# SyncE's queue in a recurrent delta-rule stage: kn is stored ahead of beta and loaded ahead of v's stores

## Chip, core and metric

The kernel runs on one core of one Trainium2 chip. The metric is the device time of one execution in microseconds (us); lower is better. Two versions are compared by the medians of their timed runs on the same chip.

## What is computed

A stack of four layers on x of 8 sequences, 256 tokens and 128 features. Each layer is a conditioning step, an attention-like step, a second conditioning step and a feed-forward step, with residual additions. The change lies in the attention-like step of layer 2, a recurrent delta rule with 8 heads of 32, which is fed by an LSTM and followed by a plain RNN. Cut to what matters:

```python
def _L2_attn_ref(x, W_in, W_k, W_v, W_q, W_beta, b_beta, W_out):
    xp = silu(einsum('btd,ed->bte', x, W_in))
    k_all, v_all, q_all = proj(W_k), proj(W_v), proj(W_q)
    beta_all = sigmoid(proj(W_beta) + b_beta)
    def step(S, inp):
        k, v, q, beta = inp
        kn = k / (norm(k) + 1e-06)
        retrieved = einsum('bhij,bhj->bhi', S, kn)
        delta = v - retrieved
        S = tanh(beta[..., None] * S + delta[..., None] * kn[..., None, :])
        Sq = einsum('bhij,bhj->bhi', S, q)
        return S, Sq * silu(Sq)
    S_final, outs = scan(step, S0, (k_all, v_all, q_all, beta_all))
    return einsum('btm,dm->btd', cell_out, W_out)

x = x + _L2_attn_ref(_L2_cond_ref(x, cond, ...), ...)      # LSTM, then the delta rule
x = x + _L2_ffn_ref(_L2_cond2_ref(x, cond, ...), ...)      # plain RNN, then a ternary feed-forward
```

## The kernel before

The program goes through its stages one after the other; all weights lie in SBUF. The stage of the change is `recurrent_stages` (tensor names begin with `l2r_`). It runs three recurrences side by side, each delayed against the one that feeds it. Time is cut into 16 waves of `TC` = 16 steps, and a loop over bodies works on five waves at once (`waves`, L349):

- wave k of the LSTM (`lstm_products`, `lstm_gates`, `lstm_cell`), one step per step of the body;
- wave k-1 of `project`: from the LSTM's output it makes k, v, beta and q of 16 steps in one go, spread over the steps of the body;
- wave k-2 of the delta recurrence: `values` and `retrieve` (L415, L429) put v minus the retrieved value into `d_ps` on TensorE; `masked` (L800) copies it to `rows` on VectorE; `spread_delta` (L441) multiplies it with `outer`, which holds kn, into `o_ps`; `kept` (L649) makes beta times state on GpSimd; `summed` (L808) adds both into `pre` on VectorE; `new_state` (L556) takes the tanh on ScalarE. Each waits for the one before it, so a step is a ring through four engines;
- wave k-3 of the output projection and wave k-4 of the RNN.

TensorE also does matmuls whose result nobody reads (`unread`, L448), a fixed number in each step.

Each engine's instruction order is written out by hand: the code of a step of the body stands in one fixed order on each engine, and every engine executes its own list in order.

k, v and beta come out of `project` with the token (sequence and step) on the partition axis, and the recurrence needs the head and the sequence there. They are turned round through device memory by SyncE's DMA queue. For wave w of `project`, this is:

- `store_beta` (L939): 8 DMAs of 16 KB, from `beta_tok`, once ScalarE's sigmoid of beta (L592, step 9 of the body) is done;
- `store_kn` (L948): 2 DMAs of 64 KB, from `kn_tok`, once GpSimd's multiply (L702, step 9 of the body too) is done;
- `store_v` (L968): 2 DMAs of 96 KB, from `v_part`, in rows of 32 bf16 elements;
- `load_kn` (L957): 4 DMAs of 32 KB to `kn_rows`, once both kn stores have landed. ScalarE multiplies them by a mask into `outer` (L612), four instructions in steps 13 to 15 of the same body, ahead of that step's `new_state`;
- `load_beta` (L927): 16 DMAs of 256 KB to `beta_f`, in four parts of four. The first part and half of the second follow in the same body, the rest in the next, each paced by the step in which its ring slot comes free;
- `load_v` (L976): 1 DMA of 192 KB to `v_rows`, once both v stores have landed. TensorE's `values` of the next body's step 0, at the end of this body, waits for it.

Before this, at the start of each body, SyncE issues the remaining beta loads of the wave that the delta recurrence is in. A wait of a function stands on SyncE ahead of its DMAs and holds up all that is queued behind it.

Of the kernel before, what the change touches and what calls it, by code (L numbers as in the profile page):

```python
# [260 lines left out]
def recurrent_stages(nc, tag, x, y, wx, wh, bias, w_in, w_tok, w_q, beta_bias, w_out, sel_v, mask_r, mask_k, mask_q, mask_l, gate_sel,  # L261
# [8 lines left out]
    with ExitStack() as stack:  # L270
# [78 lines left out]
        def waves(k):  # L349
            return [w if 0 <= w < NTC else None for w in (k, k - 1, k - 2, k - 3, k - 4)]  # L350

        with nc.Block() as block:
# [562 lines left out]
            def _(sp):  # L915
                def load_beta(w, part, chunks, delta=None, step=0):
                    q = w * (TC // QUARTER) + part
                    sp.wait_ge(s["beta_stored"], 16 * B * (w + 1))
                    if q >= BETA_SLOTS:
                        sp.wait_ge(s["bs_ready"], (q - BETA_SLOTS + 1) * QUARTER * 2)  # L920
                        sp.wait_ge(beta_loaded[q % BETA_SLOTS], 16 * 4 * (q // BETA_SLOTS))
                    for m in chunks:
                        if delta is not None and delta * TC + step >= 1:
                            sp.wait_ge(s["bs_ready"], 2 * (delta * TC + step))
                        step += 1
                        here = beta_store[w % 2, :, m, part * QUARTER:(part + 1) * QUARTER].rearrange("g t h b i -> g (t h b i)")
                        sp.dma_start(beta_f[chunk_rows(m), q % BETA_SLOTS].rearrange("p g t h b i -> p g (t h b i)"),  # L927
                                     here.unsqueeze(0).broadcast_to([32, HG, QUARTER * 2 * BH * N2])).then_inc(beta_loaded[q % BETA_SLOTS], 16)

                def store_beta(w):  # L930
                    sp.wait_ge(s["beta_done"], w + 1)
                    if w >= 2:
                        for slot in range(BETA_SLOTS):
                            last = ((w - 1) * (TC // QUARTER) - 1 - slot) // BETA_SLOTS + 1
                            sp.wait_ge(beta_loaded[slot], 16 * 4 * last)
                    if w >= 1:
                        sp.wait_ge(s["beta_stored"], 16 * B * w)
                    for b in range(B):
                        sp.dma_start(beta_store[w % 2, :, :, :, b // BH, b % BH, :].rearrange("g m t i -> t (g m) i"),  # L939
                                     beta_tok[TC * b:TC * (b + 1), :].rearrange("p (c i) -> p c i", i=N2)  # L940
                                     ).then_inc(s["beta_stored"], 16)

                def store_kn(w):
                    sp.wait_ge(s["kn_ready"], w + 1)
                    if w >= 1:
                        sp.wait_ge(s["kn_loaded"], 16 * 4 * w)
                    for h in range(2):
                        sp.dma_start(kn_store[h].rearrange("m b t j -> (b t) m j"), kn_tok[BH * TC * h:BH * TC * (h + 1), :, :]  # L948
                                     ).then_inc(s["kn_stored"], 16)

                def load_kn(w):
                    sp.wait_ge(s["kn_stored"], 16 * 2 * (w + 1))
                    if w >= 1:
                        sp.wait_ge(s["outer_ready"], 4 * w)
                    for c in range(4):
                        h, g = divmod(c, 2)
                        sp.dma_start(kn_rows[32 * c:32 * c + 16, :, :].rearrange("p t j -> p (t j)"),  # L957
                                     kn_store[h, 4 * g:4 * (g + 1)].rearrange("m b t j -> (m b) (t j)")
                                     ).then_inc(s["kn_loaded"], 16)

                def store_v(w):
                    sp.wait_ge(s["top_ready"], w + 1)
                    sp.wait_ge(s["mid_ready"], w + 1)
                    sp.wait_ge(s["v_split"], w + 1)
                    if w >= 1:
                        sp.wait_ge(s["v_loaded"], 16 * w)
                    for h in range(2):
                        sp.dma_start(v_store[:, h].rearrange("r b t i -> (b t) r i"),  # L968
                                     v_part[BH * TC * h:BH * TC * (h + 1), :, :].rearrange("p a (m i) -> p (a m) i", i=N2)
                                     ).then_inc(s["v_stored"], 16)  # L970

                def load_v(w):
                    sp.wait_ge(s["v_stored"], 16 * 2 * (w + 1))
                    if w >= 2:
                        sp.wait_ge(s["d_psum"], (w - 1) * TC)
                    sp.dma_start(v_rows[0:V_ROWS, w % 2, :, :, :].rearrange("p b t i -> p (b t i)"),  # L976
                                 v_store.rearrange("r h b t i -> (r h) (b t i)")).then_inc(s["v_loaded"], 16)

                for k in range(1, NTC + 2):
                    lstm, proj, delta, out, rnn = waves(k)  # L980
                    if delta is not None:
                        load_beta(delta, 1, (2, 3), delta, 0)
                        load_beta(delta, 2, range(4), delta, 2)
                        load_beta(delta, 3, range(4), delta, 6)
                    if proj is not None:
                        store_beta(proj)
                        store_kn(proj)
                        store_v(proj)
                        load_kn(proj)
                        load_beta(proj, 0, range(4), delta, 10)  # L990
                        load_v(proj)
                        load_beta(proj, 1, (0, 1), delta, 14)
# [2233 lines left out]
```

## Time and profile before

| | |
|---|---|
| median of 3 runs | 2966.37 us (2957.95 to 2966.97) |
| the profiled execution's own time | 2981.45 us |
| its span | 2979.7 us |
| mean granted clock of TensorE in it, as a share of full speed | 0.821 |
| busy: PE, DVE, ACT, POOL | 2485.5, 1725.2, 1105.3, 750.8 us |
| SyncE's beta, kn and v stores: first and last issue | 1310.4 and 2070.2 us |

The profile names engines PE (TensorE matmul), PEld (TensorE weight load), DVE (VectorE), ACT (ScalarE), POOL (GpSimd) and SP (SyncE). A row of a timeline merges neighbouring instructions of one line and gives their start, their length together, and in square brackets the idle time of the engine before them with what ended it. For DMAs the length is that of issuing them on SyncE's queue, and "to landing" is the time from an issue to its semaphore. The stage lies between about 1250 and 2180 us of the span.

### The profile page before, as it was taken

How to read it: one execution, taken by the hardware profiler on the slowest of the kernel's cores; microseconds unless marked ns; L12 is line 12 of the kernel's file. 1: busy time of each engine (PE TensorE's matmuls, PEld its weight loads, DVE VectorE, ACT ScalarE, POOL GpSimd, SP SyncE). 2: the span in 40 equal slices, each digit the busy share in tenths (PEclk: the TensorE clock that was granted, in tenths of full speed). 3: DMA queues.
4: the chain of work that ended last, by engine and by line, in shares of the span. 5: the costliest groups of instructions: out<-in, count | busy, mean ns of one | idle time of the engine just before them, and what ended most of it. 6: DMA issues, size and time to landing. Idle time of an engine off the chain costs nothing. (4 is left out here: it accounts for less than half of the span.)

```text
span 2979.7 us, 92693 instructions
## 1 busy us (share of the span) xinstructions
PE 2485.5 (83%) x37349; PEld 1762.4 (59%) x37354; DVE 1725.2 (58%) x7330; ACT 1105.3 (37%) x3986; POOL 750.8 (25%) x1227
## 2 busy tenths in 40 slices
PE   5998888882799889778888888889956878999998
PEld 3556666662455566555666666665534556777774
DVE  3553555556354544347777877776343865566675
ACT  1332333333133223224555555555244433333332
POOL 2210000000221000126666666767333310000000
PEclk9996555555699779889999999999556975898999
DMA  2000000001000000123534343435010000000000
GB/s 89 2 3 2 2 2 2 2 2 39 1 2 2 1 0 0 67 48 92 111 95 108 97 106 98 107 96 115 30 43 1 2 1 2 2 3 2 2 3 15
DMA packets 110106, 103.98 MB, mean 35 GB/s; under 512 B 90496, under 2 KB 90496, under 8 KB 108800
## 3 DMA queue, kind: packets, MB, share of 16 engines
q1 hardware_dynamic: 109696, 98.24, 13.1%
q8 instruction: 291, 4.77, 0.7%
q14 instruction: 119, 0.97, 0.1%
HBM read 89.81 MB, written 8.39 MB: 33 GB/s over the span
## 5 line engine op out<-in xcount | busy, mean ns | idle before, releaser
L649 POOL TENSOR_TENSOR l2r_beta_s<-l2r_state,l2r_beta_f 128x256 f32<-128x256 f32 x512 | 366.1, 736 | 274.8 <-ACT l2r_state L556 265.4
L556 ACT ACTIVATE l2r_state<-l2r_pre 128x256 f32<-128x256 f32 x512 | 191.6, 417 | 220.3 <-DVE l2r_pre L808 218.6
L808 DVE TENSOR_TENSOR l2r_pre<-l2r_o_ps,l2r_beta_s 128x256 f32<-128x256 f32 x512 | 193.1, 418 | 35.2 <-PE l2r_o_ps L441 33.1
L140 PE MATMUL l0r_bank<-main_x,l0r_wx_half 128*128 128x32 f32 (+2 forms) x480 | 150.0, 413 | 60.5 <-ACT l0r_out_gate L196 59.9
L140 PEld LDWEIGHTS l0r_bank<-main_x,l0r_wx_half 128*128 128x128 f32 x480 | 118.7, 311 | 81.7 <-ACT l0r_out_gate L196 79.5
L1801 PEld LDWEIGHTS l3r_bank<-main_x,l3r_wx_half 128*128 128x128 f32 x480 | 98.1, 231 | 93.2 <-issue 49.4
L441 PE MATMUL l2r_o_ps<-l2r_rows,l2r_outer 32*128 32x128 f32 x2048 | 134.1, 333 | 4.6 <-DVE l2r_rows L800 4.1
L194 ACT ACTIVATE l0r_gates<-l0r_bank 128x24 f32<-128x24 f32 x256 | 48.9, 191 | 237.0 <-PE l0r_bank L152 237.0
L1940 ACT ACTIVATE l3r_gates<-l3r_bank 128x24 f32<-128x24 f32 x256 | 48.9, 191 | 232.2 <-PE l3r_bank L1813 232.1
L228 DVE SCALAR_TENSOR_TENSOR l0r_both<-l0r_gates 128x16 f32<-128x16 f32 x256 | 44.8, 175 | 152.4 <-ACT l0r_gates L194 152.4
L152 PE MATMUL l0r_bank<-l0r_h_ring,l0r_w_part 128*128 128x8 bf16 x2304 | 102.6, 170 | 35.7 <-DVE l0r_h_ring L238 28.0
L1784 POOL TENSOR_SCALAR main_y<-l3r_h_ring 128x128 f32<-128x128 f32 x16 | 8.5, 530 | 481.9 <-DVE l3r_h_ring L2094 481.9
L152 PEld LDWEIGHTS l0r_bank<-l0r_h_ring,l0r_w_part 128*128 128x128 bf16 x2304 | 81.5, 105 | 68.4 <-DVE l0r_h_ring L238 65.0
L124 POOL TENSOR_SCALAR main_y<-l0r_h_ring 128x128 f32<-128x128 f32 x16 | 10.3, 645 | 441.8 <-DVE l0r_h_ring L238 441.8
L800 DVE TENSOR_TENSOR l2r_rows<-l2r_d_ps,main_even_layers 128x128 f32<-128x128 f32 x257 | 74.8, 291 | 80.5 <-PE l2r_d_ps L429 75.4
L448 PE MATMUL l2r_d_ps<-l2r_w_part 128*128 128x384 bf16 x384 | 120.8, 359 | 0.0
L441 PEld LDWEIGHTS l2r_o_ps<-l2r_rows,l2r_outer 32*128 32x128 f32 x2048 | 83.5, 191 | 55.5 <-DVE l2r_rows L800 48.0
L429 PE MATMUL l2r_d_ps<-l2r_state,l2r_kq 128*32 128x128 f32 x2056 | 114.2, 284 | 1.6 <-ACT l2r_state L556 1.4
L2084 DVE SCALAR_TENSOR_TENSOR l3r_both<-l3r_gates 128x16 f32<-128x16 f32 x256 | 44.4, 173 | 114.1 <-ACT l3r_gates L1940 113.3
L1314 DVE TENSOR_REDUCE l1a_block_top<-l1a_s_ps 128x6 f32<-128x768 f32 x64 | 61.3, 958 | 83.1 <-PE l1a_s_ps L1167 83.1
L1801 PE MATMUL l3r_bank<-main_x,l3r_wx_half 128*128 128x32 f32 (+2 forms) x480 | 95.9, 295 | 15.4 <-ACT l3r_out_gate L1942 14.8
L1314 DVE TENSOR_REDUCE l0a_block_top<-l0a_s_ps 128x6 f32<-128x768 f32 x64 | 61.3, 958 | 79.6 <-PE l0a_s_ps L1167 79.6
(590 smaller groups left out, 7305.4 us busy)
## 6 DMA issues: line engine op xcount, KB each, us to landing
l2r_beta_f<-l2r_beta_store SPq DMA_DIRECT2D x256, 256.0 KB, 3.3
main_odd_layers<-in_l SPq DMA_DIRECT2D x1, 4826.5 KB, 14.1
main_odd_layers<-in_l SPq DMA_DIRECT2D x1, 3672.0 KB, 16.3
l2r_v_store<-l2r_v_part SPq DMA_DIRECT2D x32, 96.0 KB, 3.5
l2r_v_rows<-l2r_v_store SPq DMA_DIRECT2D x16, 192.0 KB, 7.0
main_decay<-in_decay SPq DMA_DIRECT2D x1, 3072.0 KB, 10.2
main_even_layers<-in_l SPq DMA_DIRECT2D x1, 2762.5 KB, 9.7
l2r_beta_store<-l2r_beta_tok SPq DMA_DIRECT2D x128, 16.0 KB, 1.6
```

The costliest lines, as they stand in the source:

```text
L140: nc.tensor.matmul(into, wx_half[:, g * P:(g + 1) * P], x_b[:, :, w * LW + lo:w * LW + hi].rearrange("p b t -> p t b"), start=False, stop= ...
L152: last = nc.tensor.matmul(ifg(n, at, at + 1), w_part[part][:, g * P:(g + 1) * P], h_parts[k], start=False, stop=(k == 2), skip_group_check ...
L194: nc.scalar.activation(gates[:, 0:3 * B], ifg(n), ACT.Tanh).then_inc(s["gates_ready"], 1)
L429: last = nc.tensor.matmul(d_ps[chunk_rows(c), 0:P], kq[:, n % SLOTS, c, :, :, :].rearrange("p a b c -> p (a b c)"), state[:, c * P:(c + 1) ...
L441: last = nc.tensor.matmul(o_ps[:, c, 0:P], outer[chunk_rows(c), n // TC % 2, n % TC, :, :].rearrange("p a b -> p (a b)"), rows[chunk_rows( ...
L448: nc.tensor.matmul(into[:, P:CHUNK], w_part[0][:, 0:P], w_part[0][:, 0:3 * P], start=True, stop=True)
L556: nc.scalar.activation(state[:, h * 2 * P:(h + 1) * 2 * P], pre[:, h * 2 * P:(h + 1) * 2 * P], ACT.Tanh).then_inc(state_ready[h], 1)
L649: nc.gpsimd.tensor_tensor(beta_s[:, half].rearrange("p (g r) -> p g r", g=HG), state[:, half].rearrange("p (g r) -> p g r", g=HG), beta_f[ ...
L800: nc.vector.tensor_tensor(rows[:, n % SLOTS, :, :].rearrange("p a b -> p (a b)"), d_ps[:, 0:P], mask_r, ALU.mult).then_inc(s["row_ready"], 1)
L808: nc.vector.tensor_tensor(pre[:, half].rearrange("p (c n) -> p c n", c=2), o_ps[:, 2 * h:2 * h + 2, 0:P], beta_s[:, half].rearrange("p (c ...
L1314: nc.vector.tensor_reduce(block_top[:, :, 2 * p:2 * p + 2, r].rearrange("p n g -> p g n"), s_ps[:, :, 0:SPAN].rearrange("p g (n k) -> p g ...
L1801: nc.tensor.matmul(into, wx_half[:, g * P:(g + 1) * P], x_b[:, :, w * LW + lo:w * LW + hi].rearrange("p b t -> p t b"), start=False, stop= ...
```

## The change

In SyncE's loop over the bodies the kn stores stand ahead of the beta stores, and the kn loads stand ahead of the v stores. Nothing else is changed; each function keeps its waits.

```diff
                     if proj is not None:
+                        store_kn(proj)
                         store_beta(proj)
-                        store_kn(proj)
+                        load_kn(proj)
                         store_v(proj)
-                        load_kn(proj)
                         load_beta(proj, 0, range(4), delta, 10)
                         load_v(proj)
                         load_beta(proj, 1, (0, 1), delta, 14)
```

On SyncE, in body 1 (wave 0's projection, the first of the stage), the difference of the two instruction lists is:

```order
 L914 UNCONDITIONAL_BRANCH
+L948 DMA l2r_kn_store<-l2r_kn_tok 64x8x32 x2
 L939 DMA l2r_beta_store<-l2r_beta_tok 16x8x32 x8
-L948 DMA l2r_kn_store<-l2r_kn_tok 64x8x32 x2
+L957 DMA l2r_kn_rows<-l2r_kn_store 16x512 x4
 L968 DMA l2r_v_store<-l2r_v_part 64x24x32 x2
-L957 DMA l2r_kn_rows<-l2r_kn_store 16x512 x4
 L927 DMA l2r_beta_f<-l2r_beta_store 32x2x1024 x4
 L976 DMA l2r_v_rows<-l2r_v_store 48x2048
 L927 DMA l2r_beta_f<-l2r_beta_store 32x2x1024 x12
```

The kn stores moved past the eight beta stores, and the kn loads past the two v stores. The v stores now stand directly ahead of beta's first four loads. The same piece repeats in all 16 bodies that project a wave. In the last of them, body 16, SyncE's list before is:

```order
L939 DMA l2r_beta_store<-l2r_beta_tok 16x8x32 x8
L948 DMA l2r_kn_store<-l2r_kn_tok 64x8x32 x2
L968 DMA l2r_v_store<-l2r_v_part 64x24x32 x2
L957 DMA l2r_kn_rows<-l2r_kn_store 16x512 x4
L927 DMA l2r_beta_f<-l2r_beta_store 32x2x1024 x4
L976 DMA l2r_v_rows<-l2r_v_store 48x2048
```

and after it:

```order
L948 DMA l2r_kn_store<-l2r_kn_tok 64x8x32 x2
L939 DMA l2r_beta_store<-l2r_beta_tok 16x8x32 x8
L957 DMA l2r_kn_rows<-l2r_kn_store 16x512 x4
L968 DMA l2r_v_store<-l2r_v_part 64x24x32 x2
L927 DMA l2r_beta_f<-l2r_beta_store 32x2x1024 x4
L976 DMA l2r_v_rows<-l2r_v_store 48x2048
```

Here too the v load is the last of the wave's six groups that the next body waits for. The lists of TensorE, VectorE, ScalarE and GpSimd are the same in both kernels.

## Rows read from the trace of the kernel before

**Rows 1.** The page, its first line.
```profile
span 2979.7 us, 92693 instructions
```

**Rows 2.** Waits of ScalarE, then of SyncE's queue: us in total, times, longest us.
```profile
ACT l2r_outer L612 <- DMA l2r_kn_rows<-l2r_kn_store: 12.0, 9, 3.3
...
SPq L957 <- DMA l2r_kn_store<-l2r_kn_tok: 1.3, 4, 0.8
```

**Rows 3.** Timeline of SyncE in wave 8's projection: start us, us, DMAs.
```profile
1714.18 3.77 SPq L939 DMA_DIRECT2D l2r_beta_store<-l2r_beta_tok  x8
1718.05 1.27 SPq L948 DMA_DIRECT2D l2r_kn_store<-l2r_kn_tok  x2
1719.48 1.48 SPq L968 DMA_DIRECT2D l2r_v_store<-l2r_v_part  x2
1721.06 3.18 SPq L957 DMA_DIRECT2D l2r_kn_rows<-l2r_kn_store  x4
1724.40 1.73 SPq L927 DMA_DIRECT2D l2r_beta_f<-l2r_beta_store  x4
1726.23 0.36 SPq L976 DMA_DIRECT2D l2r_v_rows<-l2r_v_store  x1
```

**Rows 4.** Timeline of ScalarE and GpSimd in the same wave.
```profile
1713.75 0.40 ACT L592 ACTIVATE l2r_beta_tok<-l2r_beta_tok 128x256 f32<-128x256 f32 x1
...
1714.19 0.61 POOL L702 TENSOR_TENSOR l2r_kn_tok<-l2r_k_tok,l2r_inv 128x256 f32<-128x256 f32 x1
```

**Rows 5.** Windows: us; busy PE, PEld, DVE, ACT, POOL; clock, DMA share, GB/s.
```profile
1720.00:1721.00 1.00, 0.92 (x11) 0.55 (x11) 0.79 (x5) 0.64 (x3) 1.00 (x3) 1.00 0.64 91
1721.00:1722.00 1.00, 0.74 (x25) 0.75 (x26) 0.97 (x5) 0.43 (x2) 1.00 (x3) 1.00 0.93 123
1722.00:1723.00 1.00, 1.00 (x20) 0.58 (x17) 0.84 (x3) 0.54 (x4) 1.00 (x3) 1.00 0.68 81
1726.00:1733.00 7.00, 6.34 (x122) 4.59 (x121) 4.10 (x22) 4.72 (x17) 6.37 (x10) 1.00 1.05 212
```

**Rows 6.** Lines L968, L976 (waves 8 and 2) with landings; L415 taking those v rows.
```profile
L968 SPq DMA_DIRECT2D l2r_v_store<-l2r_v_part x2: 575/716/857, 1719.5 to 1720.1; - x2
...
DMA to landing us min/median/max: 3.2/3.9/4.7
...
L976 SPq DMA_DIRECT2D l2r_v_rows<-l2r_v_store x1: 362/362/362, 1726.2 to 1726.2; - x1
...
DMA to landing us min/median/max: 7.3/7.3/7.3
...
1735.45 0.24 PE L415 MATMUL l2r_d_ps<-l2r_v_rows,l2r_selv_bf 128*32 128x128 bf16 x4
...
L976 SPq DMA_DIRECT2D l2r_v_rows<-l2r_v_store x1: 362/362/362, 1424.4 to 1424.4; - x1
...
DMA to landing us min/median/max: 7.2/7.2/7.2
...
1432.11 0.24 PE L415 MATMUL l2r_d_ps<-l2r_v_rows,l2r_selv_bf 128*32 128x128 bf16 x4
```

**Rows 7.** Timeline of ScalarE around its wait of wave 14, in body 15.
```profile
2026.53 0.75 ACT L556 ACTIVATE l2r_state<-l2r_pre 128x256 f32<-128x256 f32 x2 [0.90 <-DVE l2r_pre L808]
...
2030.16 0.72 ACT L612 ACTIVATE l2r_outer<-l2r_kn_rows,main_even_layers 128x512 f32<-128x512 f32 x1 [2.04 <-DMA l2r_kn_rows<-l2r_kn_store]
...
2030.94 0.71 ACT L556 ACTIVATE l2r_state<-l2r_pre 128x256 f32<-128x256 f32 x2
```

**Rows 8.** Timeline of TensorE: the v rows of waves 0 and 15 are taken.
```profile
1329.05 0.24 PE L415 MATMUL l2r_d_ps<-l2r_v_rows,l2r_selv_bf 128*32 128x128 bf16 x4 [1.38 <-DMA l2r_v_rows<-l2r_v_store]
...
2083.09 0.24 PE L415 MATMUL l2r_d_ps<-l2r_v_rows,l2r_selv_bf 128*32 128x128 bf16 x4 [1.62 <-DMA l2r_v_rows<-l2r_v_store]
```

**Rows 9.** Windows, columns as in rows 5: before and after the clock falls.
```profile
2073.00:2085.10 12.10, 10.34 (x118) 6.38 (x113) 4.26 (x12) 5.87 (x15) 9.25 (x15) 1.00 0.90 195
2085.20:2125.00 39.80, 39.80 (x291) 19.90 (x289) 16.52 (x44) 12.51 (x36) 16.15 (x23) 0.50 0.17 55
```

## The prediction

> **What bounds the kernel now.** I read the page first, for the span [rows 1], then the waits of ScalarE, then the DMA queue of SyncE in order of time. The profiled execution has a span of 2979.7 us and took 2981.45 us; the median of the three timed runs is 2966.37 us, 15.1 us below it. I work out a difference on the profiled execution and add it to the median. A change below 0.3% (8.9 us) can't be told from none here: the three runs alone spread over 9.0 us.
>
> The stage that changes has 20 bodies of 16 steps, about 50 us each once all waves run; body w+1 projects, stores and loads wave w. Its steps are a ring TensorE, VectorE, ScalarE, GpSimd, and SyncE only feeds it. So SyncE's order counts only where an engine of the ring waits for a transfer. I look at three such places.
>
> 1. ScalarE scales the kn rows into `outer` (L612) at step 13. It waited there 9 times in 16 waves, 12.0 us in all [rows 2]. This is the wait the change aims at. The queue itself hardly waits for the kn stores (1.3 us in 4 times, in the same group), so taking the v stores out from between store and load costs it little.
> 2. TensorE's `values` (L415), first of the next body, needs the v rows. It was held up visibly at two of the 16 loads, the first and the last [rows 8].
> 3. GpSimd's `kept` (L649) needs beta's first part.
>
> **The wave in detail, and the same wave after the change.** This is wave 8 before [rows 3]: beta stores at 1714.18, kn stores at 1718.05, v stores at 1719.48, kn loads at 1721.06, beta loads at 1724.40, v load at 1726.23. The beta stores begin as soon as beta's sigmoid (L592) ends, at 1714.15; kn_tok (L702) is ready only at 1714.19+0.61 = 1714.80 [rows 4]. With the kn stores first, the whole queue starts 0.65 us later. Then, with the same durations:
> - kn stores 1714.83 to 1716.10, beta stores 1716.20 to 1719.97 (their landing is no condition for what follows),
> - kn loads from 1720.05 instead of 1721.06, that is **1.0 us earlier** (1.48+0.11 us of v stores taken out, less 0.65 of late start), to 1723.23,
> - v stores 1723.35 to 1724.83, instead of 1719.48,
> - beta loads from 1724.95, **0.55 us later**,
> - v load after both the beta loads (1726.7) and the landing of the v stores. The second v store is issued some 0.6 us after the first and lands 3.2 to 4.7 us later [rows 6]: 1727.3 to 1728.7. So the v load leaves 1.1 to 2.5 us later than its 1726.23.
>
> No transfer, packet or instruction is added or removed, and TensorE, VectorE, ScalarE and GpSimd keep their order. The beta loads of the running wave, ahead of these, keep theirs too.
>
> **What the earlier kn loads bring.** At most the waits in [rows 2], each shortened by about 1.0. Part of each is free: where ScalarE isn't held up at L612, it waits 0.90 us for `pre` in a step, and behind the wait of wave 14 that idle time is gone [rows 7]. Wave 14 has the dearest that isn't tied to the v load: 2.04 us, and its step took 2030.94-2026.53 = 4.41 us [rows 7]; two steps later the pace was normal. Of the 1.0 us I count 0.9. Wave 4 (1.17 us) I count at 0.2, the waits below 0.9 us at nothing. In wave 0, the first, L612 waited 3.26 us, but the body ends with TensorE waiting 1.38 us for v rows at 1329.05 [rows 8], so a faster ScalarE only waits longer there; there the queue starts no later, since kn_tok is ready first, and I count 0.1. In wave 1 the v rows are as close behind, see below. **Gain: 1.2 us.** Its bounds are 0 (every wait hidden) and 8.5 us (1.0 us or the whole wait in each of the nine, all on the path; about 3 us of it from wave 0).
>
> **What the later v and beta loads cost.** The beta loads and the v load keep the DMA engines full: a share of 1.05 in the 7 us from 1726 [rows 5]. The v rows of wave 8 land 7.3 us after their issue [rows 6], at 1733.5, behind beta's. TensorE takes them at 1735.45: 1.9 us to spare. In wave 2 they land at 1424.4+7.2 = 1431.6, and are taken at 1432.11: 0.5 us to spare [rows 6]. Read the same way, the loads of waves 1, 3 and 4 have 0.6 to 0.7, wave 7 has 0.9, the other nine between 1.3 and 2.4, and waves 0 and 15 none.
>
> How much later do they land? Beta's loads are issued 0.55 us later. Besides, the v stores' packets now lie directly ahead of them. Before, these took the engines at shares of 0.64, 0.93 and 0.68 in the three microseconds after 1720 [rows 5], 2.25 us of all sixteen, and were gone when beta's data came, because the kn loads lay between. After, v's data run from some 0.7 to 3.5 us after their issue, 1724.0 to 1726.8, and beta's would begin 1.1 us after its issue, at 1726.0. What is left of v's data then is about a third of them, 0.7 us. So the v rows land 0.55+0.7 = **1.25 us later**. Bounds: 0.55 (no queueing) and 2.8 (0.55 and all 2.25). I take the lower half because most of v's data drain while beta's loads are being issued.
>
> The Trainium skill (DMA: Bandwidth & Descriptors, Anatomy of one DMA) fits a transfer issued by GpSimd as about 2.0 us and its bytes at 436 GB/s; for two v stores of 96 KB each that would be 0.45 us of engine time. The 2.25 us [rows 5] speak against it here, at 64 bytes a packet. By the page nothing of v would be left in beta's way, the shift would be 0.55 us and the whole sum about 0.
>
> With 1.25 us, wave 1 is 0.6 late, wave 2 0.7, waves 3 and 4 0.5 each, wave 7 0.3: 2.6 us. Wave 14, sped up by its kn gain, finds its v rows late and gives back 0.5. Wave 15 already waits, 1.62 us [rows 8], so there the shift counts in full, with its stores also in the way: 1.4 us. **Cost: 4.5 us.** Beta's first part would be late only with 1.5 us or more; it is covered by v, which lands behind it.
>
> **Sum:** -1.2+4.5 = +3.3 us, so about **2970 us**.
>
> **The clock.** TensorE's granted clock is full (2.4 GHz) through the stage and fell to half (1.2 GHz) at body 17, the last with a delta: 1.00 before 2085.1, 0.50 in the 40 us behind it [rows 9], just behind the wait of 1.62 us for wave 15's v rows. The changed kernel makes that wait longer, so I expect the same fall, at most a few microseconds earlier. If some of the timed runs keep full clock there, the change can cost them that. I charge nothing.
>
> **The rivals.**
> - *The v rows come late in nearly every wave* (slower). If v's 64-byte packets keep beta's data back by more than I take, or land late and so delay the v load's own issue, the shift passes 1.9 us. Then six or more further waves lose their slack. At 2.2 us the sum is about +14 us: **2981 us**. It counts as slower from a shift of 1.9 us on (+9 us). For it: a v store took up to 4.7 us to land [rows 6], and the engines are full. Against it: the waves with 1.3 to 2.4 us to spare. Chance 0.20.
> - *ScalarE's wait is on the path* (faster). If a held-up ScalarE delays the ring one for one and the v rows land no later, 8.5 us go: **2958 us**. For it: 4.41 us for the step of wave 14. Against: the 0.90 us of slack [rows 7], which covers four of the nine waits whole. Chance 0.08, of which I give 0.06 to faster by over 0.3%.
> - *It does nothing:* kn lands 1.0 us earlier where nobody waits, v lands later within its slack. **2966 us**. For it: 14 of 16 v loads have slack now. Chance 0.25.
> - The forecast, a few microseconds lost at waves 1 to 4 and 15: 0.47.
>
> **The numbers.** Faster 0.06; slower 0.20; the rest, 0.74, is within 0.3%. The range takes in the faster rival's 2958 below (also the fastest run shown) and the slower one's 2981 above: 2958 to 2982.
>
> **What would show it.** In the profile after: SyncE's first kn store of wave 8 about 0.65 us behind the end of L592, kn loads about 1.0 us earlier and beta loads about 0.5 us later against L592; ScalarE's wait at L612 down from 12.0 to between 2 and 5 us; L415 waiting for the v rows at five to seven loads, not two, 0.3 to 1.5 us each; bodies 5 to 13 as long as before to within 0.7 us. I am wrong if the v rows land more than 2 us later, if bodies get shorter by 0.5 us or more, or if another stage changes.

## The result, and the profile after

| | kernel before | changed kernel |
|---|---|---|
| median of 20 runs each | 2959.79 us | 2977.18 us |
| ratio of the changed kernel to the kernel before | | 1.0071, 95% interval 1.005 to 1.0093 |
| the profiled execution: its own time, its span | 2981.45, 2979.7 us | 2975.27, 2973.4 us |
| mean granted clock of TensorE in it | 0.821 | 0.822 |

The change makes the kernel slower by 0.7%: 21 us by the ratio (15 to 28 by its interval), 17.4 us by the medians. Ratios and the counts further down leave out the executions more than 1.5% above the fastest of their kernel (5938.07 and 3004.14 us of the kernel before and 3881.32 us of the changed one here, three more of the kernel before and one of not15 later). The forecast was 2970 us; 2977.18 us lies inside the stated range, but on the side to which I gave a chance of 0.20. And the two profiled executions show the opposite: the one of the changed kernel is 6 us shorter. Each number of this section has to be read with that in mind.

The queue of SyncE first, in the changed kernel, wave 8 again, with the engine rows that release it. Columns: start us, us, what.

```profile
1712.01 0.40 ACT L592 ACTIVATE l2r_beta_tok<-l2r_beta_tok 128x256 f32<-128x256 f32 x1
...
1713.09 1.27 SPq L948 DMA_DIRECT2D l2r_kn_store<-l2r_kn_tok  x2
1714.53 3.82 SPq L939 DMA_DIRECT2D l2r_beta_store<-l2r_beta_tok  x8
1718.45 2.99 SPq L957 DMA_DIRECT2D l2r_kn_rows<-l2r_kn_store  x4
1721.60 1.49 SPq L968 DMA_DIRECT2D l2r_v_store<-l2r_v_part  x2
1723.25 2.22 SPq L927 DMA_DIRECT2D l2r_beta_f<-l2r_beta_store  x4
1726.20 0.31 SPq L976 DMA_DIRECT2D l2r_v_rows<-l2r_v_store  x1
```

Counted from the start of L592, the queue begins at 1.08 us instead of 0.43 [rows 3, 4], the kn loads at 6.44 instead of 7.31, the beta loads at 11.24 instead of 10.65, the v load at 14.19 instead of 12.48. So the kn loads leave 0.9 us earlier, the beta loads 0.6 us and the v load 1.7 us later, all close to what was worked out. This v load took 7.0 us to land, so the v rows came 1.4 us later.

The waits of ScalarE and TensorE for DMAs in the changed kernel (us in total, times, longest us):

```profile
PEld l2r_d_ps L415 <- DMA l2r_v_rows<-l2r_v_store: 9.8, 5, 4.4
PE l2r_d_ps L415 <- DMA l2r_v_rows<-l2r_v_store: 8.2, 4, 4.1
...
ACT l2r_outer L612 <- DMA l2r_kn_rows<-l2r_kn_store: 1.7, 2, 1.0
```

The 12.0 us of ScalarE [rows 2] are down to 1.7, in 2 waves instead of 9. TensorE now waits for v rows at five loads: its matmuls at four (waves 0, 1, 11 and 15), and a weight load (PEld) alone at wave 14, for 0.37 us. What that makes of the stage is seen from the delta recurrence's tanh (L556), whose row gives its first and last start; before, then after:

```profile
L556 ACT ACTIVATE l2r_state<-l2r_pre x512: 399/417/428, 1331.2 to 2141.5; 128x256 f32<-128x256 f32 x171
```

```profile
L556 ACT ACTIVATE l2r_state<-l2r_pre x512: 416/417/424, 1328.3 to 2141.5; 128x256 f32<-128x256 f32 x171
```

That is 810.3 us and 813.2 us: 2.9 us more, where the sum of the prediction said 3.3. The other 9 us between the two spans lie outside the recurrence. So in this pair of executions the sum comes out (by which terms is looked at further down), and the 21 us of the runs are not to be seen in it. The reason stands in the two rows of the changed kernel that answer to [rows 8, 9]:

```profile
2081.88 0.24 PE L415 MATMUL l2r_d_ps<-l2r_v_rows,l2r_selv_bf 128*32 128x128 bf16 x4 [2.36 <-DMA l2r_v_rows<-l2r_v_store]
```

```profile
2085.20:2125.00 39.80, 39.80 (x291) 19.85 (x289) 16.23 (x43) 12.35 (x36) 16.15 (x23) 0.50 0.17 54
```

TensorE waits 2.36 us instead of 1.62 for wave 15's v rows, and behind it the clock is at half (1.2 GHz), as in [rows 9]. The first question was therefore whether [rows 9] show what the kernel before usually does: its profiled execution took 2981.45 us, 22 us more than the median of 20 runs.

### The profile page after: what moved, and what is told of

Read it like the earlier page. It is cut to its first block and busy times, and to the rows that moved or that the text cites. A ratio compares the mean times of both kernels' runs of the same rounds, so it can differ in the third digit from the quotient of the medians.

```text
span 2973.4 us, 92698 instructions
## 1 busy us (share of the span) xinstructions
PE 2481.7 (83%) x37354; PEld 1760.2 (59%) x37354; DVE 1726.2 (58%) x7330; ACT 1105.8 (37%) x3986; POOL 750.7 (25%) x1227
## 5 line engine op out<-in xcount | busy, mean ns | idle before, releaser
L556 ACT ACTIVATE l2r_state<-l2r_pre 128x256 f32<-128x256 f32 x512 | 192.1, 418 | 231.7 <-DVE l2r_pre L808 229.7
L124 POOL TENSOR_SCALAR main_y<-l0r_h_ring 128x128 f32<-128x128 f32 x16 | 10.3, 645 | 439.3 <-DVE l0r_h_ring L238 439.3
## 6 DMA issues: line engine op xcount, KB each, us to landing
main_odd_layers<-in_l SPq DMA_DIRECT2D x1, 3672.0 KB, 16.2
```

Source lines behind the costliest of these rows:

```text
L556: nc.scalar.activation(state[:, h * 2 * P:(h + 1) * 2 * P], pre[:, h * 2 * P:(h + 1) * 2 * P], ACT.Tanh).then_inc(state_ready[h], 1)
```

## The experiments

Two theories. **Clock:** most executions of the kernel before keep full clock through body 17, since TensorE's wait for wave 15's v rows is short enough; the change makes this wait longer, so the clock is lost nearly always. **Queue:** the v rows come late in many waves, and the pair of traces happens not to show it (my slower rival).

Each experiment comes with 12 runs, against 33 to 35 runs of the kernel before on the same chip, in three sets (to fill15, to load15, the rest). The last column counts the executions whose mean granted clock is 0.827 or lower: among the traces, the highest mean with the clock lost in body 17 is 0.827, the lowest with it kept is 0.828. Only the traced executions show where the clock fell; for the others the mean is a sign of it, and with so narrow a gap a count can be off by one or two.

| kernel | median us | ratio to before, 95% interval | low mean clock |
|---|---|---|---|
| before (three sets) | 2956.52, 2958.2, 2953.45 | | 21 of 102 |
| the change | 2977.18 | 1.0071 (1.005 to 1.0093) | 19 of 19 |
| b_again | 2958.74 | 1.0014 (0.9987 to 1.0042) | 3 of 12 |
| only15 | 2978.19 | 1.0071 (1.0044 to 1.0097) | 11 of 12 |
| not15 | 2963.9 | 1.0006 (0.9979 to 1.0032) | 3 of 11 |
| fill15 | 2957.71 | 0.9994 (0.9972 to 1.0017) | 0 of 12 |
| after_fill15 | 2964.15 | 1.0015 (0.9994 to 1.0036) | 1 of 12 |
| idle15 | 2973.36 | 1.0039 (1.0013 to 1.0066) | 9 of 12 |
| store15 | 2972.3 | 1.0036 (1.001 to 1.0062) | 9 of 12 |
| load15 | 2976.05 | 1.0051 (1.002 to 1.0083) | 12 of 12 |
| vfirst15 | 2955.01 | 0.9985 (0.996 to 1.0009) | 0 of 12 |
| fill_0_15 | 2946.84 | 0.9972 (0.9948 to 0.9995) | 0 of 12 |
| new0_fill | 2947.26 | 0.9969 (0.9947 to 0.9991) | 0 of 12 |
| after_fill_all | 2953.26 | 0.9983 (0.9957 to 1.0008) | 0 of 12 |

**b_again: a second trace of the kernel before.** No edit.

> The kernel before once more, unchanged, for a second trace. Its three first times and its profiled one (2981 us) lie 15 us apart. Clock theory: in a typical execution TensorE keeps full clock in body 17 (the last delta body), and its steps take about 2.7 us there, not 3.57 as in the trace shown; then this profile shows it, if its own time is near 2960 us. Queue theory (the loss of the change sits in v rows that come late in many waves): body 17 looks as in the first trace, at half clock, whatever the time. Both: ratio to before 1.00 within 0.3%.

Its profiled execution took 2950.37 us, 31 us less than the first. Three rows of it: the taking of wave 15's v rows, a window of 40 us in body 17 (columns as in rows 5), and the tanh.

```profile
2073.05 0.24 PE L415 MATMUL l2r_d_ps<-l2r_v_rows,l2r_selv_bf 128*32 128x128 bf16 x4 [0.59 <-DMA l2r_v_rows<-l2r_v_store]
```

```profile
2075.50:2115.50 40.00, 37.69 (x408) 20.49 (x408) 20.98 (x56) 16.22 (x48) 22.16 (x32) 1.00 0.19 58
```

```profile
L556 ACT ACTIVATE l2r_state<-l2r_pre x512: 403/417/428, 1324.1 to 2115.6; 128x256 f32<-128x256 f32 x171
```

The wait is 0.59 us instead of 1.62, the clock stays at 1.00, and 40 us hold 408 matmuls instead of 291 in 39.8 us. The recurrence takes 791.5 us, 18.8 us less than in the first trace of the same program. Most of that is body 17: from its first tanh to its last it takes 40.05 us instead of 55.85, at 2.67 us a step instead of 3.57. So the kernel has two courses, and the profile before the change showed the rarer one (21 of 102). The timed runs put the same price on it: in the three sets the median of the kernel before's executions with a low mean clock lies 18.6, 19.0 and 16.2 us above that of its others.

**only15 and not15: where the loss sits.** The new order in body 16 alone, or in all bodies but that:

```diff
-                    if proj is not None:
+                    if proj is not None and proj == 15:
+                        store_kn(proj)
                         store_beta(proj)
-                        store_kn(proj)
-                        store_v(proj)
                         load_kn(proj)
+                        store_v(proj)
+                    elif proj is not None:
...
```

> The new order of SyncE's queue in body 16 alone (wave 15's projection), the old one in all others. Clock theory: this alone lengthens TensorE's wait for wave 15's v rows from 1.6 to about 3 us and so costs the clock of body 17 nearly always: nearly the whole loss, +12 to +20 us. Queue theory: +1 to +2 us, the shift of one v load.

> The new order in all bodies but body 16. Clock theory: +0 to +6 us, the late v rows of wave 1 and a few others and the half clock behind them in body 3. Queue theory: +15 us or more, the whole loss but for one load.

One body out of 16 carries the loss as far as the intervals can tell: 1.0071 like the change itself, while the other 15 give 1.0006 (at most 1.0032, or 9.5 us). The taking of wave 15's v rows in only15, and 40 us of body 17:

```profile
2076.15 0.30 PE L415 MATMUL l2r_d_ps<-l2r_v_rows,l2r_selv_bf 128*32 128x128 bf16 x4 [3.12 <-DMA l2r_v_rows<-l2r_v_store]
```

```profile
2079.60:2119.60 40.00, 40.00 (x291) 19.84 (x289) 16.44 (x44) 12.55 (x37) 16.15 (x23) 0.50 0.18 54
```

The queue theory in its form of many late waves falls here. What remained open was whether the lateness or the idle TensorE does it.

**idle15: more idle time without a later transfer.** SyncE's queue as before; in the last step of body 16 the three matmuls that nobody reads are left out.

```diff
-                        for _ in range(UNREAD[lstm is not None, delta is not None]):
+                        for _ in range(0 if n == 239 else UNREAD[lstm is not None, delta is not None]):
```

> The old order of SyncE's queue. The three matmuls that nobody reads in the last step of body 16 are left out (nothing that is computed changes), so TensorE idles 0.6 us more ahead of wave 15's values, while the v rows come as before. Clock theory: the clock is lost in most runs, +12 to +20 us. Rival (late v rows themselves): no change.

Less work and no transfer moved, and yet it is 0.39% slower (about 12 us, the lower end of what was expected), with 9 of 12 executions at a low mean clock. Those nine took 2967.38 to 2980.03 us, the other three 2948.51 to 2963.95. Its profiled execution is one of the three: it waited just 0.61 us there, and kept the clock. The v rows came 0.4 us sooner in it than in b_again's (taken 2.96 us after those of the step before, not 3.35), so the added idle time doesn't show in this trace; that the nine lost the clock in body 17 rests on their times and mean clocks.

```profile
2069.96 0.24 PE L415 MATMUL l2r_d_ps<-l2r_v_rows,l2r_selv_bf 128*32 128x128 bf16 x4 [0.61 <-DMA l2r_v_rows<-l2r_v_store]
...
2072.50:2112.50 40.00, 37.68 (x408) 20.49 (x408) 20.98 (x56) 16.23 (x48) 22.18 (x32) 1.00 0.19 60
```

**fill15 and after_fill15: the late transfer without the idle time.** Matmuls that nobody reads, ahead of wave 15's values, 10 in the kernel before and 20 in the changed one. They only fill a wait.

```diff
+                        for _ in range({240: 10}.get(n + 1, 0)):
+                            unread(d_ps)
                         if delta is not None and n + 1 < T:
                             values(n + 1)
```

> The old order, and 10 more of the matmuls that nobody reads on TensorE at the end of body 16, ahead of wave 15's values, where it waited 1.6 us for the v rows. The result stays the same. Clock theory: TensorE doesn't idle there, keeps full clock into body 17 in more of the runs; 0 to -8 us, and a smaller spread of the times, if the idle time is what decides it. Queue theory: no change (the ten take 1.6 us that were idle), 0 to +1 us.

> The changed kernel, and 20 of the matmuls that nobody reads (0.16 us each, 3.3 us) on TensorE ahead of wave 15's values, where it waited about 3 us for the v rows. Clock theory: the v rows come as late as in the changed kernel, but the clock stays up through body 17 in most runs: +1 to +5 us against before instead of +21. A rival, that it is the later v rows and what queues behind them in SyncE's list that cost the time: +17 us or more still.

The changed kernel with 20 fillers is at 1.0015 instead of 1.0071: about four fifths of the loss are gone, and about half at the upper end of its interval (1.0036), though no transfer comes earlier. Its trace has the lateness without the price. Body 16, up to the first tanh of body 17, takes 46.6 us (46.7 in the changed kernel, 45.0 and 44.0 in the two traces of the kernel before); body 17, from its first tanh to its last, takes 40.04 us (56.13 in the changed kernel). With 10 of them in the kernel before, the median stays and the slow tail goes: 2951.58 to 2966.88 us, where before's own runs of that set reached 2984.06. Of after_fill15, 40 us of body 17:

```profile
2090.00:2130.00 40.00, 37.69 (x414) 20.40 (x411) 21.03 (x55) 16.15 (x47) 20.55 (x30) 1.00 0.20 64
```

**store15 and load15: the two halves of the change, in body 16 alone.**

```diff
+                    if proj is not None and proj == 15:
+                        store_kn(proj)
+                        store_beta(proj)
+                        store_v(proj)
+                        load_kn(proj)
...
```

and for load15 the order `store_beta`, `store_kn`, `load_kn`, `store_v`.

> In body 16 alone, the kn stores ahead of the beta stores, the kn loads left behind the v stores. The queue starts 1.1 us later there, since kn_tok is ready later than beta in this body, and nothing else moves: v rows about 1 us later, wait about 1.6 us instead of 0.6 in an execution like that of b_again. Clock theory: it is enough to lose the clock in most runs, +8 to +18 us. Rival: +1 us.

> In body 16 alone, the kn loads ahead of the v stores, the stores of beta and kn in the old order. The v stores' packets lie right ahead of the beta loads, and the v load waits for their landing: v rows 0.5 to 1.2 us later. Clock theory: the clock is lost in about half of the runs or more, +5 to +15 us. Rival: +1 us.

Either half suffices to lose the clock in most executions (9 and 12 of 12). The waits in their traces were 1.82 us (store15) and 1.23 us (load15), both with the clock lost:

```profile
2074.22 0.24 PE L415 MATMUL l2r_d_ps<-l2r_v_rows,l2r_selv_bf 128*32 128x128 bf16 x4 [1.82 <-DMA l2r_v_rows<-l2r_v_store]
```

```profile
2083.32 0.24 PE L415 MATMUL l2r_d_ps<-l2r_v_rows,l2r_selv_bf 128*32 128x128 bf16 x4 [1.23 <-DMA l2r_v_rows<-l2r_v_store]
```

In store15's trace TensorE had also idled 1.85 us for the state, 7 us before, so that trace doesn't set the two waits apart. For load15 the expectation said about half of the runs or more; it was 12 of 12.

**vfirst15: the v rows earlier instead.** In body 16 the v load goes ahead of the first four beta loads.

```diff
+                        if proj == 15:
+                            load_v(proj)
                         load_beta(proj, 0, range(4), delta, 10)
-                        load_v(proj)
+                        if not (proj == 15):
+                            load_v(proj)
```

> The old order of stores and kn loads; in body 16 alone wave 15's v load goes ahead of the first four beta loads instead of behind them. Clock theory: the v rows land several us earlier, TensorE doesn't idle for them (but perhaps, for about 1 us, for the state behind beta), fewer runs lose the clock than before: 0 to -5 us. Rival (only the lateness counts): -1 us.

No execution has a low mean clock. The median can't be told from before (0.9985), but the longest of 12 runs is 2961.11 us, against 2978.85 of before's in that set. In its trace TensorE doesn't wait for wave 15's v rows, and body 17 takes 40.03 us. It is the opposite move to the change, and it removes what the change made certain.

**fill_0_15, new0_fill and after_fill_all: can both be beaten, and what is left of the loss?** fill_0_15 adds 8 fillers ahead of wave 0's values to the 10 of fill15. new0_fill takes the new order in body 1 alone, with 24 and 10 fillers. after_fill_all is the changed kernel with 20, 5 and 20 fillers ahead of the values of waves 0, 1 and 15:

```diff
+                        for _ in range({16: 5, 240: 20}.get(n + 1, 0)):
+                            unread(d_ps)
                         if delta is not None and n + 1 < T:
                             values(n + 1)
...
                         if n == 0:
+                            for _ in range(20):
+                                unread(d_ps)
                             values(0)
```

> The old order; matmuls that nobody reads fill TensorE's wait for the v rows both ahead of wave 0's values (8) and of wave 15's (10). A candidate for faster than both kernels. Clock theory: full clock in the first delta body too, where steps of 4.4 to 4.8 us ran at half clock: -3 to -6 us against before.

> The new order in body 1 alone (wave 0), the old one elsewhere, with 24 unread matmuls ahead of wave 0's values (where the changed kernel waited 4.1 us) and 10 ahead of wave 15's. The second candidate. Clock theory: as fill_0_15, and 0.2 to 1 us more from wave 0's earlier v rows: -3 to -7 us.

> The changed kernel in full, with unread matmuls ahead of the values of waves 0 (20), 1 (5) and 15 (20). Clock theory: what after_fill15 still lost (0.15%) was the half clock in bodies 2 and 3 behind waves 0 and 1, so with it filled the new order costs nothing that can be measured: -3 to +3 us against before. Rival: the late v rows of the other waves cost +5 us or more.

fill_0_15 and new0_fill are faster than the kernel before by 0.3%, and so faster than both kernels; the new order in body 1 adds nothing that the intervals can tell. after_fill_all, with all 16 waves in the new order, can't be told from the kernel before (0.9983). So once TensorE's clock is held, the new order itself costs nothing that can be measured, and the saved 10 us of ScalarE's waiting bring nothing that can be measured either. In the trace of after_fill_all the clock stays full from 1290 to 2120 us, past the last tanh. The candidates gave somewhat more than expected, -8 and -9 us by the ratios instead of -3 to -6 and -3 to -7; their intervals (-1.5 to -15 and -3 to -16 us) take in what was expected. after_fill_all gave -5 us (-13 to +2), where -3 to +3 was expected.

## Why the prediction was right and wrong

**The queue.** Right in every shift of wave 8: late start 0.65 us, kn loads 1.0 said and 0.9 measured, beta loads 0.55 and 0.6, v rows 1.25 and 1.4. But wave 8 doesn't stand for all waves. The v rows landed 7.0 us after issue in the changed kernel's wave 8 and a median of 6.3 over all 16, against 7.0 before:

```profile
L976 SPq DMA_DIRECT2D l2r_v_rows<-l2r_v_store x16: 312/313/361, 1319.4 to 2074.9; - x16
...
DMA to landing us min/median/max: 5.5/6.3/7.5
```

In the median this gives back 0.7 us of the 1.7. Counted from the start of L592 of the same wave, the v rows landed between 1.0 us earlier and 2.0 us later than in the trace before, 0.5 us later in the mean, where 1.25 was said for every wave. That a load which leaves later finds less ahead of it is my reading; no run sets it apart. The 2.25 us of engine time that the shift was worked out from weren't v's alone either: the three rows moved 295 KB (91, 123 and 81 GB/s for 1 us each, [rows 5]), and the v stores are 192 KB.

**The kn gain.** Sized at 1.2 us, bounds 0 and 8.5 (the nine waits cut by at most 1.0 us each give 6.9, not 8.5). ScalarE's wait fell by 10.3 us, to 1.7, below the 2 to 5 us that the prediction named as its sign. after_fill_all (0.9983, 0.9957 to 1.0008) leaves the gain and the cost of late v rows together near nothing. So nearly all of the saved wait lay off the path, as forecast.

**The late v rows in the other waves.** Forecast at waves 1 to 4, 7, 14 and 15. TensorE waited at five loads, within the five to seven forecast, but at other ones: not at waves 2, 3, 4 and 7, where 2.0 us had been charged and the v rows had 0.9 to 1.7 us to spare, more than before; and at wave 11, by 0.75 us, where nothing had been:

```profile
1886.09 0.24 PE L415 MATMUL l2r_d_ps<-l2r_v_rows,l2r_selv_bf 128*32 128x128 bf16 x4 [0.75 <-DMA l2r_v_rows<-l2r_v_store]
```

The sum of +3.3 us was 2.9 us against the execution that it was made against, but by other terms. Counted from the first tanh of one body to that of the next, body 2 is 2.5 us shorter (its stretch at half clock ends sooner: 50.5 us instead of 52.9), body 3 is 3.9 us longer, body 12 0.7 us, body 16 1.7 us (1.4 were said for wave 15), and body 15 is 1.1 us shorter; bodies 5 to 13 agree within the 0.7 us that the prediction allowed. Body 2 alone takes 49.9 to 54.4 us in the eight traces in which waves 0 and 1 have the old order and no filler, and body 15 49.1 to 50.2 us in those with the old order there, so that the agreement of 3.3 and 2.9 is luck in the main. What is long in body 3 is a second stretch at half clock, behind wave 1's late v rows:

```profile
1378.80:1392.50 13.70, 13.62 (x162) 8.64 (x159) 8.30 (x36) 4.20 (x18) 4.23 (x6) 0.51 0.24 70
```

I had not forecast that. not15, without wave 15, is at 1.0006, so that all of this together is small. A long wait isn't a cost by itself either: ahead of wave 0's values it grew from 1.38 to 4.06 us, but the v rows were taken 18.8 us after the start of L592 instead of 19.1. TensorE was ready sooner and waited for the rest.

**The step that failed** is the paragraph on the clock: "I expect the same fall ... I charge nothing." It named the place, the wait and the direction, and even the loss ("If some of the timed runs keep full clock there, the change can cost them that"), and gave it no price. It took [rows 9] for the usual course. The runs show that the kernel before loses the clock there in 21 of 102 executions, the changed one in 19 of 19. At 16 to 19 us for a loss (the runs of the three sets, and body 17 in the two traces of the kernel before) that is 0.79 times as much, 13 to 15 us; with the 3 us of the sum it is 16 to 18 us, of 17 by the medians and 21 by the ratio.

There were two signs in what the prediction had before it: a profiled execution 15 us above the median, which it noted and passed over, and a clock that fell 2 us behind a wait of 1.62 us. A price could have been worked out from the same trace too: body 17 went at 3.57 us a step at half clock, body 16 at 2.67 at full clock; for 16 steps that is some 14 us.

**The rivals.** The slower rival had the right side and, by luck, nearly the right size (2981 us), and the wrong mechanism: one late transfer of 16 did it, by the clock, not many late ones. The faster one and "it does nothing" fall with 1.0071.

The Trainium skill (TensorE: Matmul & The Clock Gate, What's actually happening) says that the point at which the clock changes isn't tied to the kernel's start and varies from run to run; the low mean clock of 21 in 102 equal executions agrees. The same page (HAM oscillation) describes matmul groups that each lose the clock in a wait for a DMA of some 3 to 5 us. The six traces here that lost it ahead of body 17 agree in kind, but five of the six waits were shorter, 1.12 to 2.36 us.

## What to carry to other kernels

Before costing a change on one profile, compare that execution's time with the median of the runs: a gap of 15 us of which no term of the sum speaks means that the profile may show another course than most runs take. Where a trace shows TensorE's clock falling behind a wait, price the clock of the whole stretch that follows, not the wait; test it by adding idle time with no other change, and by filling the wait with matmuls that nobody reads. A transfer with slack in 14 of 16 waves can have its whole price in one that has none (here wave 15; wave 0 had none either and cost nothing that was seen), so moving work past it there and not elsewhere is a different change.

## What the runs showed of the hardware

- Waits of TensorE ahead of body 17 and its clock behind them: 0.59 and 0.61 us, kept (b_again, idle15); filled, kept (fill15, after_fill15); 1.12 us (not15), 1.23, 1.62, 1.82, 2.36 and 3.12 us, lost. The trace of not15 for the shortest wait that lost it:

```profile
2081.02 0.24 PE L415 MATMUL l2r_d_ps<-l2r_v_rows,l2r_selv_bf 128*32 128x128 bf16 x4 [1.12 <-DMA l2r_v_rows<-l2r_v_store]
```

- The length of a wait alone doesn't decide. In not15 the clock fell to half behind this wait for wave 1's v rows (0.52 in the 2 us from 1378), while in the changed kernel it stayed full behind the equally long one of wave 11:

```profile
1377.92 0.24 PE L415 MATMUL l2r_d_ps<-l2r_v_rows,l2r_selv_bf 128*32 128x128 bf16 x4 [0.75 <-DMA l2r_v_rows<-l2r_v_store]
```

- A wait for a DMA isn't needed either. In after_fill15's trace the clock fell near 1644 us, in the middle of the stage, where TensorE had been busy 4.44 of 5 us and its longest idle time was 0.56 us; it was 0.50 from 1645 to 1650 and back at full soon after. That body took 53.2 us instead of 50.6.
- Once lost, the clock didn't come back in body 17, though TensorE was busy 39.80 of 39.80 us there [rows 9], and yet at full clock the same program kept it with 37.69 of 40.00 us busy. In bodies 2 and 3 it did come back, within some 10 to 25 us. Why it holds or returns in one case and not in the other wasn't tried.
- The same v load of the same program landed with 0.59 us of waiting in one execution and 1.62 in another. What sets this spread was not tried either.
